# Graph and expert layers on one core: one long fill behind every four row sends, shared units five a step, batch norm on ScalarE

## The chip, the cores and the metric

The kernel runs on one core of one Trainium2 chip. The metric is the device time of one execution in microseconds (us). Five engines work side by side, each with its own instruction stream: TensorE (PE; its weight loads are shown apart as PEld), VectorE (DVE), ScalarE (ACT), GpSimd (POOL) and SyncE (SP). They meet through semaphores: an instruction waits until a semaphore has reached a count, and when it is done it raises one.

## What is computed

Two layers work on a stream of 8192 tokens of 128 numbers (128 batches of 64 nodes), each with a graph part and a feed-forward part. Cut to what matters:

```python
x = x + _L0_gnn_ref(_layernorm(x), adj, ...)      # eigenvectors of a 64x64 Laplacian
x = x + _L0_ffn_ref(_layernorm(x), ...)           # top 2 of 8 experts, silu gate
x = x + _L1_gnn_ref(_layernorm(x), adj, ...)      # batch norm over all tokens, twice
x = x + _L1_ffn_ref(_layernorm(x), ...)           # shared expert + top 2 of 8, gelu

# end of _L1_gnn_ref
out = h @ W2.T + b2
out = _batchnorm(out, g2, be2)
# _L1_ffn_ref
shared = gelu(x @ W1s + b1s) @ W2s + b2s
return shared + routed
```

## The kernel before

All arithmetic is float32. The tokens are kept in SBUF as 64 columns of 128 tokens (N = 64); four columns make a tile (PAIRS = 4, 512 tokens), so there are TILES = 16 tiles. Everything is written out by hand for each engine, with counted semaphores; no scheduler moves anything, so the order of an engine's code is its order on the chip.

The program runs in stages. First the eigenvectors of the Laplacian are found (to about 290 us of the profile). Then comes the graph part of layer 0, `gnn0_*`, to about 430 us; the experts of layer 0, `experts_*`; the graph part of layer 1 up to its first and second batch norm, `mix_*` and `out_*`; then `gnn1_*`, from about 870 to 1071 us; and the experts of layer 1, with the last stores.

**Routing and sends.** During `gnn0_*` and `gnn1_*` the tokens are normalised, their router logits are made, and a `Router` picks two experts for each token. It works on groups of GQ = 8 columns, two tiles, so there are GROUPS = 8 groups in each layer. `choose` and `place` on DVE give every token its row in a list in DRAM that is sorted by expert. `scatter` on POOL then sends the group: eight indirect DMAs (`send`, L1017), one for each column, of 128 rows of 1040 bytes. Behind every two sends stands a fill, a memset of a buffer `idle` that nobody reads (128x200 numbers, REST = 200, L1013). It raises `route_rested`, and each fill first waits for the fill before it. In the last group of layer 0 no fill stands between the eight sends, one stands behind them. When all 64 sends of a layer have landed, SP loads the rows expert by expert (L1482).

**Between the graph part and the experts of layer 0** PE has little to do: it sums the counts (`sum_counts`, L1098), runs five matmuls whose result nobody reads (`keep_warm`, L1409), spreads the limits of the routing table (`spread_limits`, L1105), runs six more, waits for the fill behind the last send, runs five more, and then turns the first rows of the experts (`turn_in`, L1641).

**`gnn1_*` goes in steps**, one for each tile, and then some more. In step s:

- DVE applies the second batch norm to tile s+1 of `OUT1` (`affine`, L1995, out `mgm`, semaphore `a1_gm`), adds the transposed tile s to the tokens (L2016), and works out the mean and inverse root of each token (`row_stats`, `inverse_root`, L2033). Among these it does `choose` or `place` of a group, and for the first EARLY = 4 tiles it adds the shared expert's result (`add_shared`, L2002).
- PE transposes the batch-normed tile s (L1919), transposes the normalised tile s-1 (L1936), makes its logits (L871), and works off shared units between these, in thirds.
- ACT normalises tile s (L1963), copies the transposed tile s-1 out of PSUM (L1974), and does the units' gelu (L1896).

A shared unit is one eighth of the shared expert for one tile. Four of the eight are *up* (one 128x512 product, L1875, followed by a gelu on ACT), four are *down* (four 128x128 products, L1882). There are 128 units; eight are kept for the gap in the middle of the experts, and 120 are done in `gnn1_*`, RATE = 6 in each step, from step 2 on: units 6(s-2) to 6(s-1). That makes A1_STEPS = 22 steps (0 to 21). A *down* unit needs its gelu, and an *up* unit needs the gelu of the unit two before it.

The sends of group g can start in step 2g+5; those of groups 0 and 1 also need the shared results of their tiles to be added.

Of the kernel before, what the change touches and what calls it, by code (L numbers as in the profile page):

```python
# [8 lines left out]
ALU = mybir.AluOpType  # L9
ACT = mybir.ActivationFunctionType  # L10
# [722 lines left out]
TILES = 16  # L733
PAIRS = 4
TOK = PAIRS * P
# [6 lines left out]
GQ = 8  # L742
REST = 200
GROUPS = N // GQ
# [87 lines left out]
def per_q(ap):  # L832
# [4 lines left out]
ROUTED = dict(lg=TILES, lg_free=GROUPS, carried=GROUPS, rank=GROUPS, slots=2 * GROUPS, shift=GROUPS, gap=GROUPS, exp=2 * GROUPS,  # L837
              picked=GROUPS, gates=GROUPS, rested=GQ // 2 * (GROUPS - 1) + 1, total=1, limits=1, limit_row=1, first=1)
SENT = 16 * N
# [8 lines left out]
class Router:  # L848
# [149 lines left out]
    def scatter(self, pool, g, xs, ready):  # L998

        pool.wait_ge(self.s("slots"), self.past("slots", 2 * (g + 1)))  # L1000
        pool.wait_ge(self.s("gates"), self.past("gates", (g + 1) * (1 + self.layer)))
        ready(g)
        for k in range(GQ // 2):
            for q in range(g * GQ + 2 * k, g * GQ + 2 * k + 2):
                self.send(q, xs).then_inc(self.s("sent"), 16)
            n = GQ // 2 * g + k
            if self.layer == 0 and g == GROUPS - 1:
                if k + 1 < GQ // 2:
                    continue
                n = GQ // 2 * g  # L1010
            if n or self.layer:
                pool.wait_ge(self.s("rested"), self.past("rested", n))
            self.nc.gpsimd.memset(self.t["idle"], 0.0).then_inc(self.s("rested"), 1)  # L1013

# [391 lines left out]
def keep_warm(nc, t, bank, n):  # L1406

    for _ in range(n):
        nc.tensor.matmul(bank[:, :], t["ident"], t["spin"], start=True, stop=True)  # L1409
# [422 lines left out]

RATE = 6
EARLY = 4
HELD = 1
UNITS = 2 * CH1 * TILES
AHEAD = UNITS - 2 * CH1 * HELD
A1_STEPS = 2 + -(-AHEAD // RATE)
PLACED = TILES + 2


def units(s):

    return range(max(0, RATE * (s - 2)), min(AHEAD, max(0, RATE * (s - 1))))


def thirds(todo):

    n = -(-len(todo) // 3)
    return todo[:n], todo[n:2 * n], todo[2 * n:]  # L1850
# [55 lines left out]
def gnn1_pe(nc, pe, S, t, ps, route):  # L1906
    T = nc.tensor
# [5 lines left out]
    for s in range(A1_STEPS):  # L1913
# [11 lines left out]
        if s == PLACED + 3:  # L1925
            route.spread_limits(pe)
        begin, middle, end = thirds(units(s))
        for n in begin:
# [18 lines left out]
def gnn1_act(nc, act, S, t, ps, route):  # L1947
    A = nc.scalar
# [4 lines left out]
    def keep(n):  # L1953
        i, k, rising, c = unit(n)
        if i >= EARLY and k == 2 * CH1 - 1:
            keep_shared(nc, act, S, t, ps, i)

    def normalised(T):
        if T >= TILES:
# [5 lines left out]
        ins.then_inc(S("a1_xh"), 1)  # L1965

    for s in range(A1_STEPS):
        begin, middle, end = thirds(units(s))
        for n in begin:
# [9 lines left out]
        for n in end:  # L1979
            gelu(n)  # L1980
        normalised(s)
        for n in units(s - 1):
            keep(n)
# [4 lines left out]
def gnn1_dve(nc, dve, own, S, t, ps, route):  # L1988
    V, X = nc.vector, t["X"]

    def affine(T):

        if T >= 2:
            dve.wait_ge(S("a1_t1"), T - 1)
        V.tensor_scalar(t["mgm"][T % 2], t["OUT1"][:, T * TOK:(T + 1) * TOK], t["bn2"][:, 0, 0:1], t["bn2"][:, 1, 0:1],  # L1995
                        ALU.mult, ALU.add).then_inc(S("a1_gm"), 1)

# [9 lines left out]

    dve.wait_ge(S("bn2_ready"), 1)
    affine(0)
    for s in range(A1_STEPS):  # L2010
        if s + 1 < TILES:
            affine(s + 1)
        if s < TILES:
# [78 lines left out]
def build(nc, d, out, tokens_out, scratch):  # L2092

    with ExitStack() as ctx:
# [134 lines left out]
        def _(pe):  # L2229
# [3 lines left out]
            routes[0].sum_counts(pe)  # L2233
            keep_warm(nc, t, ps[2], 5)
            routes[0].spread_limits(pe)
            keep_warm(nc, t, ps[2], 6)
            pe.wait_ge(S("route_rested"), GQ // 2 * (GROUPS - 1) + 1)
            keep_warm(nc, t, ps[2], 5)
            experts_pe(nc, pe, S, views[0], ps, 0)
# [98 lines left out]
```

## Time and profile before

| | us |
|---|---|
| median of 3 runs | 1388.89 |
| lowest and highest | 1387.36, 1392.39 |
| the profiled execution | 1388.02 |
| its span, first to last instruction | 1385.8 |
| PE busy in the span | 1137.4 (82%) |
| DVE busy | 922.1 (67%) |
| ACT busy | 565.5 (41%) |
| POOL busy | 511.5 (37%) |

The span is what the profile covers; 2.2 us of the profiled execution lie around it. Times in rows are us from the start of the span. Busy times count an engine's work, not its waits. A row's last part in brackets is how long the engine stood idle before it, and what released it: another engine's instruction, "issue" (nothing that the profile shows), or "remote", which is also called "another core or an unknown queue" (a semaphore that rose at a time that no instruction's end explains).

### The profile page before, as it was taken

To read this page: it belongs to the slowest core of one execution; us is meant where nothing else is said; L and a number is where in the kernel's file an instruction comes from. 1 tells how busy PE (TensorE), PEld (TensorE's weight loads), DVE (VectorE), ACT (ScalarE), POOL (GpSimd) and SP (SyncE) were. 2 spreads that over 40 slices of the span, in tenths; PEclk is the share of its full clock that TensorE was granted. 3 is DMA by queue.
4 is the path that set the end of the run, shared out by engine and by line. 5 is a ranking of instruction groups with operands and counts; after the bars stand their busy time and mean duration, and the time that the engine had idled before them with its cause. 6 is when DMAs were issued, how large, how long until landed. Compare 5 with 4: busy or idle time off the path is not lost.

```text
span 1385.8 us, 25378 instructions
## 1 busy us (share of the span) xinstructions
PE 1137.4 (82%) x7088; PEld 954.0 (69%) x7088; DVE 922.1 (67%) x3893; ACT 565.5 (41%) x1720; POOL 511.5 (37%) x586
## 2 busy tenths in 40 slices
PE   3555677268875999999999999796778999999992
PEld 3555577146653888978889654574556999989991
DVE  5777688858675566756668697884632566746673
ACT  2556657215540222212222367453433444544451
POOL 2100000053566345434444450025552455535561
PEclk9999999999886999999999999898979999999996
DMA  9999990000113334323232520001112344233326
GB/s 218 427 428 427 426 388 8 0 0 24 70 70 108 125 124 126 111 68 101 93 95 62 158 112 12 3 32 62 62 62 93 117 141 138 73 113 114 107 62 190
DMA packets 78348, 178.49 MB, mean 129 GB/s; under 512 B 11736, under 2 KB 51683, under 8 KB 75392
## 3 DMA queue, kind: packets, MB, share of 16 engines
q0 software_dynamic: 20544, 112.80, 20.5%
q1 hardware_dynamic: 51328, 60.92, 15.9%
q10 hardware_dynamic: 6336, 3.15, 0.8%
q8 instruction: 58, 0.95, 0.3%
q14 instruction: 82, 0.67, 0.2%
HBM read 60.91 MB, written 119.08 MB: 130 GB/s over the span
## 4 chain that ended last, share of the span: by engine, by line
PE 63%; DVE 16%; issue 10%; another core or an unknown queue 3%; ACT 3%; POOL 1%; DMA 1%; SPq 1%; DVEq 0%; POOLq 0%; ACTq 0%
PE bank L1669 17%; PE bank L1655 16%; PE bank L1658 6%; PE bank L195 4%; PE bank L1875 3%; PE bank L1882 3%; PE bank L1641 2%; PE bank L1818 2%; PE bank L1409 1%; PE bank L871 1%; DVE bnh L1719 1%; DVE u L180 1%; DVE u L171 1%; DVE u L166 1%
## 5 line engine op out<-in xcount | busy, mean ns | idle before, releaser
L1655 PE MATMUL bank<-work,wide 128*128 128x256 f32 (+3 forms) x994 | 215.4, 330 | 3.8 <-issue 2.3
L1669 PE MATMUL bank<-wide,work 128*128 128x128 f32 x1512 | 216.5, 278 | 1.1 <-DVE work L1591 1.0
L1669 PEld LDWEIGHTS bank<-wide,work 128*128 128x128 f32 x1512 | 198.0, 191 | 10.6 <-DVE work L1591 4.2
L1017 POOL DMA_INDIRECT rows<-tokens,slot x128 | 126.8, 990 | 172.8 <-issue 95.5
L1612 ACT ACTIVATE work<-bank 128x256 f32<-128x256 f32 (+1 forms) x216 | 82.7, 383 | 264.2 <-PE bank L1658 237.3
L1655 PEld LDWEIGHTS bank<-work,wide 128*128 128x128 f32 (+1 forms) x994 | 154.1, 186 | 16.8 <-DVE wide L1527 3.4
L1506 POOL DMA_INDIRECT rows<-wide x100 | 105.6, 1056 | 127.1 <-DVE wide L1543 105.9
L195 PE MATMUL bank<-u 63*64 63x2 f32 (+61 forms) x496 | 73.7, 255 | 66.3 <-DVE u L180 65.3
L195 PEld LDWEIGHTS bank<-u 63*64 63x64 f32 (+61 forms) x496 | 64.4, 217 | 71.8 <-DVE u L180 70.5
L1591 DVE TENSOR_TENSOR work<-work,bank 128x256 f32<-128x256 f32 (+1 forms) x216 | 87.9, 417 | 38.8 <-ACT work L1612 34.7
L1527 DVE COPY wide<-wreg 128x1066 f32 (+1 forms) x142 | 100.7, 709 | 16.4 <-issue 13.1
L1658 PE MATMUL bank<-work,wide 128*128 128x256 f32 (+3 forms) x426 | 105.3, 329 | 0.0
L1882 PE MATMUL bank<-wreg,work 128*128 128x128 f32 x512 | 72.8, 292 | 29.3 <-ACT work L1896 23.3
L1882 PEld LDWEIGHTS bank<-wreg,work 128*128 128x128 f32 x512 | 67.0, 204 | 40.9 <-ACT work L1896 29.6
L1621 ACT ACTIVATE work<-bank,wide 128x256 f32<-128x256 f32 x148 | 65.3, 475 | 73.1 <-PE bank L1655 71.0
L1538 DVE COPY work<-bank 128x256 f32<-128x256 f32 x144 | 60.4, 420 | 42.0 <-PE bank L1641 24.8
L1896 ACT ACTIVATE work<-bank,wreg 128x512 f32<-128x512 f32 x64 | 43.7, 688 | 102.4 <-PE bank L1875 57.9
L1669 PE MATMUL bank<-u,work 128*128 128x128 f32 (+1 forms) x504 | 77.8, 278 | 0.4 <-DVE work L1591 0.4
L1655 PE MATMUL bank<-work,u 128*128 128x256 f32 (+1 forms) x322 | 75.2, 335 | 1.2 <-issue 1.2
L1658 PEld LDWEIGHTS bank<-work,wide 128*128 128x128 f32 (+1 forms) x426 | 69.0, 178 | 8.5
L1506 POOL DMA_INDIRECT plane<-wide x50 | 49.7, 993 | 65.4 <-DVE wide L1543 55.8
L1506 POOL DMA_INDIRECT out<-wide x50 | 52.9, 1058 | 51.4 <-DVE wide L1543 41.6
(442 smaller groups left out, 2488.0 us busy)
## 6 DMA issues: line engine op xcount, KB each, us to landing
rows<-wide POOLq DMA_DIRECT2D x20, 3432.0 KB, 97.0
wide<-rows SPq DMA_DIRECT2D x100, 260.0 KB
wide<-rows SPq DMA_DIRECT2D x88, 130.0 KB
wreg<-in_w SPq DMA_DIRECT2D x1, 4264.0 KB, 25.2
wreg<-in_w SPq DMA_DIRECT2D x1, 4112.0 KB, 14.1
tokens<-in_x SPq DMA_DIRECT2D x2, 2048.0 KB, 20.1
tokens<-plane SPq DMA_DIRECT2D x16, 256.0 KB, 5.2
tokens<-out SPq DMA_DIRECT2D x12, 256.0 KB, 6.1
```

Source lines behind the costliest of these rows:

```text
L195: T.matmul(out, A[0:rows, col:col + 1].to_broadcast([rows, N]), rhs, start=True, stop=True).then_inc(hp, 1)
L1017: return self.nc.gpsimd.indirect_dma_start(out=xs, out_offset=bass.IndirectOffsetOnAxis(ap=self.t["slot"][:, q:q + 1], axis=0), in_=self.t ...
L1506: nc.gpsimd.indirect_dma_start(out=out, out_offset=bass.IndirectOffsetOnAxis(ap=goal, axis=0), in_=t["xin"][j % RING][:, h, 0:width], in_o ...
L1527: V.tensor_copy(t["wst"][n % WAYS][:, 0:WB[layer]], W[:, bass.ds(expert * WB[layer], WB[layer])]).then_inc(s("w"), 1)
L1538: V.tensor_copy(t["xte"][j % 2], ps[6][:, 0:TS]).then_inc(s("xt"), 1)
L1591: V.tensor_tensor(t["hh"][c][0:w, :], t["hs"][c][0:w, :], ps[c][0:w, TS:2 * TS], ALU.mult).then_inc(s("hh"), 1)
L1612: A.activation(t["hs"][c][0:w, :], ps[c][0:w, 0:TS], ACT.Silu).then_inc(s("hs"), 1)
L1621: A.activation(t["hh"][c], ps[c][:, 0:TS], ACT.Gelu, bias=bias[0]).then_inc(s("hh"), 1)
L1655: ins = T.matmul(ps[c][0:n, to], w[:, a:a + n], x[:, to], start=True, stop=True)
L1658: ins = T.matmul(ps[c][0:n, to3], w[:, HID0 + a:HID0 + a + n], x[:, to], start=True, stop=True)
L1669: ins = T.matmul(ps[4 + j % 2][:, h * P:(h + 1) * P], t["hh"][c][0:n, h * P:(h + 1) * P], w[0:n, at + c * P:at + (c + 1) * P], start=(c == ...
L1882: ins = nc.tensor.matmul(ps[4 + 2 * (i % 2)][:, q * P:(q + 1) * P], t["sh"][c][:, q * P:(q + 1) * P], t["WS"][:, (CH1 + c) * P:(CH1 + c + ...
```

## The change

It has four parts.

1. **Fills.** TOGETHER = 4: a fill stands behind every four sends, and it is 128x400 (REST = 400). POOL now waits for this fill itself before it goes on. In the last group of layer 0 there is no long fill; a fill of 128x8 stands behind the sixth send, and it is the one that PE waits for.
2. **Warm matmuls of layer 0.** The five before `spread_limits` and the five behind the wait are gone; six are left, behind the wait.
3. **Shared units.** RATE = 5, and units start in step 1: units 5(s-1) to 5s. In step 1 all five stand behind the logits. A1_STEPS is 25 (0 to 24).
4. **Batch norm.** `affine` moves from DVE to ACT as an activation with scale and bias. ACT does tiles 0 and 1 before step 0, and tile s+2 behind normalising tile s.

```diff
-REST = 200
+REST = 400
+TOGETHER = 4
...
-        for k in range(GQ // 2):
-            for q in range(g * GQ + 2 * k, g * GQ + 2 * k + 2):
+        for k in range(GQ // TOGETHER):
+            for q in range(g * GQ + TOGETHER * k, g * GQ + TOGETHER * (k + 1)):
                 self.send(q, xs).then_inc(self.s("sent"), 16)
-            n = GQ // 2 * g + k
-            if self.layer == 0 and g == GROUPS - 1:
-                if k + 1 < GQ // 2:
-                    continue
-                n = GQ // 2 * g
-            if n or self.layer:
-                pool.wait_ge(self.s("rested"), self.past("rested", n))
-            self.nc.gpsimd.memset(self.t["idle"], 0.0).then_inc(self.s("rested"), 1)
+                if self.layer == 0 and q == GROUPS * GQ - 3:
+                    self.nc.gpsimd.memset(self.t["idle"][:, 0:8], 0.0).then_inc(self.s("rested"), 1)
+            if self.layer == 1 or g + 1 < GROUPS:
+                self.nc.gpsimd.memset(self.t["idle"], 0.0).then_inc(self.s("rested"), 1)
+                pool.wait_ge(self.s("rested"), self.past("rested", GQ // TOGETHER * g + k + 1))
...
-RATE = 6
+RATE = 5
...
-A1_STEPS = 2 + -(-AHEAD // RATE)
+A1_STEPS = 1 + -(-AHEAD // RATE)
...
-    return range(max(0, RATE * (s - 2)), min(AHEAD, max(0, RATE * (s - 1))))
+    return range(max(0, RATE * (s - 1)), min(AHEAD, max(0, RATE * s)))
...
+    todo = units(s)
+    n = 0 if s == 1 else -(-len(todo) // 3)
     return todo[:n], todo[n:2 * n], todo[2 * n:]
...
+    def affine(T):
+        if T >= TILES:
+            return
+        if T >= 2:
+            act.wait_ge(S("a1_t1"), T - 1)
+        A.activation(t["mgm"][T % 2], t["OUT1"][:, T * TOK:(T + 1) * TOK], ACT.Identity, bias=t["bn2"][:, 1, 0:1],
+                     scale=t["bn2"][:, 0, 0:1]).then_inc(S("a1_gm"), 1)
...
         normalised(s)
+        affine(s + 2)
...
             routes[0].sum_counts(pe)
-            keep_warm(nc, t, ps[2], 5)
             routes[0].spread_limits(pe)
+            pe.wait_ge(S("route_rested"), GQ // TOGETHER * (GROUPS - 1) + 1)
             keep_warm(nc, t, ps[2], 6)
-            pe.wait_ge(S("route_rested"), GQ // 2 * (GROUPS - 1) + 1)
-            keep_warm(nc, t, ps[2], 5)
```

POOL's order at the end of layer 0's sends and at the start of layer 1's (`rows<-tokens,slot` is a send, `idle` a fill). Before:

```order
L1017 DMA rows<-tokens,slot 67584x260 x2
L1013 MEMSET idle 128x200
L1017 DMA rows<-tokens,slot 67584x260 x8
L1013 MEMSET idle 128x200
L1506 DMA rows<-wide 67584x260 x50
```

Now:

```order
L1015 DMA rows<-tokens,slot 67584x260 x4
L1010 MEMSET idle 128x400
L1015 DMA rows<-tokens,slot 67584x260 x6
L1008 MEMSET idle 128x8
L1015 DMA rows<-tokens,slot 67584x260 x2
L1504 DMA rows<-wide 67584x260 x50
```

The fill that PE waits for stands two sends earlier, and elsewhere four sends stand in a row.

PE's order around the routing table of layer 0. Before:

```order
L1098 MATMUL bank5<-carry,consts 128x16
L1409 MATMUL bank2<-consts 128x512 x5
L1105 MATMUL bank5<-tb,consts 128x94
L1409 MATMUL bank2<-consts 128x512 x11
```

Now:

```order
L1096 MATMUL bank5<-carry,consts 128x16
L1103 MATMUL bank5<-tb,consts 128x94
L1407 MATMUL bank2<-consts 128x512 x6
```

Ten of the sixteen warm matmuls are gone, five of them from behind the limits.

ACT's order from the normalising of step 2 of `gnn1_*` to that of step 3 (L1896, now L1895, is a gelu; L1974, now L1984, the copy out of PSUM). Before:

```order
L1963 ACTIVATE tokens<-tokens,norm 128x128 x4
L1974 COPY u1<-bank1 128x512
L1896 ACTIVATE work<-bank2,wreg 128x512
L1896 ACTIVATE work<-bank3,wreg 128x512
L1896 ACTIVATE work<-bank2,wreg 128x512
L1963 ACTIVATE tokens<-tokens,norm 128x128 x4
```

Now:

```order
L1970 ACTIVATE tokens<-tokens,norm 128x128 x4
L1962 ACTIVATE work<-u1,bn2 128x512
L1895 ACTIVATE work<-bank2,wreg 128x512
L1984 COPY u1<-bank1 128x512
L1895 ACTIVATE work<-bank3,wreg 128x512
L1970 ACTIVATE tokens<-tokens,norm 128x128 x4
```

The batch norm (L1962) stands right behind the normalising, ahead of the gelus of the next step.

## Rows read from the trace of the kernel before

**Rows 1.** Chain of work, 868 to 1080 us: shares by line; start, us, what.
```profile
by line: PE bank L1875 21.2%; PE bank L1882 20.7%; another core or an unknown queue 18.9%; ACT tokens L1963 6.1%; PE bank L871 5.6%; issue 5.4%; PE bank L1936 3.3%; ACT work L1896 2.8%; PE bank L1919 2.0%; PE bank L1655 1.7%; PE bank L1669 
...
886.40 0.89 PE bank L1882 x8
887.29 0.86 PE bank L1875 x2
...
918.63 3.42 another core or an unknown queue
```

**Rows 2.** Busy us (instructions) of PE, PEld, DVE, ACT, POOL; clock, DMA share, GB/s.
```profile
926.00:937.00 11.00, 10.50 (x69) 8.03 (x68) 9.52 (x49) 5.46 (x12) 0.00 (x0) 1.00 0.03 9
...
947.00:960.00 13.00, 1.75 (x6) 0.48 (x4) 0.00 (x0) 1.16 (x3) 9.97 (x14) 0.63 0.29 104
```

**Rows 3.** PE in time: transposes that open steps 5, 6, 10, 11.
```profile
905.44 0.60 PE L1919 MATMUL bank<-consts,work 128*128 128x128 f32 x4
...
912.85 0.60 PE L1919 MATMUL bank<-consts,work 128*128 128x128 f32 x4
...
944.85 0.60 PE L1919 MATMUL bank<-consts,work 128*128 128x128 f32 x4
...
966.95 0.60 PE L1919 MATMUL bank<-consts,work 128*128 128x128 f32 x4
```

**Rows 4.** DVE in time: start, us, line, shapes, idle before and releaser.
```profile
946.10 0.68 DVE L1995 TENSOR_SCALAR work<-u,bn 128x512 f32<-128x512 f32 x1 [0.68 <-DVE norm L2034]
960.25 0.69 DVE L2016 TENSOR_TENSOR tokens<-tokens,bank 128x512 f32<-128x512 f32 x1 [13.46 <-remote]
```

**Rows 5.** POOL in time: sends (L1017) and fills (L1013) of layer 1.
```profile
914.93 1.02 POOL L1017 DMA_INDIRECT rows<-tokens,slot  x1 [43.94 <-ACT tokens L1963]
...
939.64 0.29 POOL L1013 MEMSET idle<- 128x200 f32 x1
940.09 0.97 POOL L1017 DMA_INDIRECT rows<-tokens,slot  x1 [0.17 <-issue]
941.36 0.97 POOL L1017 DMA_INDIRECT rows<-tokens,slot  x1 [0.30 <-issue]
942.33 0.29 POOL L1013 MEMSET idle<- 128x200 f32 x1
...
945.55 0.97 POOL L1017 DMA_INDIRECT rows<-tokens,slot  x1 [0.17 <-issue]
...
958.56 0.29 POOL L1013 MEMSET idle<- 128x200 f32 x1
```

**Rows 6.** DVE in time, layer 0, under sends without fills.
```profile
436.62 0.17 DVE L1072 SCALAR_TENSOR_TENSOR tb<-tb,kroute 128x16 f32<-128x16 f32 x1
437.67 0.19 DVE L1074 TENSOR_TENSOR tb<-tb 128x32 f32<-128x32 f32 x1 [0.88 <-DVE tb L1072]
```

**Rows 7.** PE in time, layer 0: limits, warm matmuls, first expert tile.
```profile
441.91 0.74 PE L1105 MATMUL bank<-tb,consts 128*128 128x94 f32 x2 [7.39 <-DVE tb L1082]
442.44 10.96 PE L1409 MATMUL bank<-consts 128*128 128x512 f32 x22
453.24 0.38 PE L1641 MATMUL bank<-consts,wide 128*128 128x128 f32 x2
```

**Rows 8.** SP in time: the first row loads of the experts.
```profile
445.78 3.64 SPq L1482 DMA_DIRECT2D wide<-rows  x4
```

**Rows 9.** Busy us per stretch, columns as in the windows above.
```profile
447.50:448.50 1.00, 1.00 (x3) 0.38 (x2) 0.31 (x1) 0.00 (x0) 0.00 (x0) 1.00 0.59 135
...
441.90:445.00 3.10, 3.09 (x5) 1.60 (x6) 0.48 (x2) 0.00 (x0) 2.01 (x3) 0.50 0.35 129
```

**Rows 10.** POOL by line: the long fill, count, busy us, mean ns.
```profile
L714 POOL MEMSET work<- 128x868 f32 x1 | 0.8, 822 | 173.6 <-DMA rows<-wide 173.6
```

**Rows 11.** Source lines: count, ns min/median/max, first and last start, form.
```profile
L1807 ACT ACTIVATE work<-u,bn x16: 797/798/801, 838.8 to 862.9; 128x512 f32<-128x512 f32 x16
...
L1995 DVE TENSOR_SCALAR work<-u,bn x16: 530/546/680, 870.7 to 995.2; 128x512 f32<-128x512 f32 x16
```

More of the change, by code:

```diff
@@ L837 @@
 ROUTED = dict(lg=TILES, lg_free=GROUPS, carried=GROUPS, rank=GROUPS, slots=2 * GROUPS, shift=GROUPS, gap=GROUPS, exp=2 * GROUPS,
-              picked=GROUPS, gates=GROUPS, rested=GQ // 2 * (GROUPS - 1) + 1, total=1, limits=1, limit_row=1, first=1)
+              picked=GROUPS, gates=GROUPS, rested=GQ // TOGETHER * (GROUPS - 1) + 1, total=1, limits=1, limit_row=1, first=1)
 SENT = 16 * N
@@ L1837, with thirds @@
 AHEAD = UNITS - 2 * CH1 * HELD
-A1_STEPS = 2 + -(-AHEAD // RATE)
+A1_STEPS = 1 + -(-AHEAD // RATE)
 PLACED = TILES + 2
 def units(s):
-    return range(max(0, RATE * (s - 2)), min(AHEAD, max(0, RATE * (s - 1))))
-def thirds(todo):
-    n = -(-len(todo) // 3)
+    return range(max(0, RATE * (s - 1)), min(AHEAD, max(0, RATE * s)))
+def thirds(s):
+    todo = units(s)
+    n = 0 if s == 1 else -(-len(todo) // 3)
     return todo[:n], todo[n:2 * n], todo[2 * n:]
@@ L1926, in gnn1_pe @@
             route.spread_limits(pe)
-        begin, middle, end = thirds(units(s))
+        begin, middle, end = thirds(s)
         for n in begin:
@@ L1965, in normalised @@
         ins.then_inc(S("a1_xh"), 1)
+    act.wait_ge(S("bn2_ready"), 1)
+    affine(0)
+    affine(1)
     for s in range(A1_STEPS):
-        begin, middle, end = thirds(units(s))
+        begin, middle, end = thirds(s)
         for n in begin:
@@ L1989, in gnn1_dve @@
     V, X = nc.vector, t["X"]
[L1991 to L1996, printed above, removed]
     def add_shared(i):
@@ L2006, in root @@
             inverse_root(V, dve, t, S("a1_inv"), s, k)
-    dve.wait_ge(S("bn2_ready"), 1)
-    affine(0)
     for s in range(A1_STEPS):
-        if s + 1 < TILES:
-            affine(s + 1)
         if s < TILES:
```

## The prediction, made before the changed kernel ran

> **What bounds the kernel now.** I read the chain of waits first, then windows, then single engines in time. The change touches three places: the sends of both layers, PE between the graph part and the experts of layer 0, and `gnn1_*`.
>
> In `gnn1_*` the chain of waits between 868 and 1080 us is mostly PE: *up* products L1875 hold 21.2%, *down* products L1882 20.7% [rows 1]. The surprise is the third entry, "another core or an unknown queue" with 18.9% of these 212 us, that is 40 us [rows 1]. It is time in which an engine waits for a semaphore whose producer has long finished. One place shows it plainly. PE ends the transposes of step 10 within 0.6 us of 944.85 [rows 3]; DVE, which waits for just these, starts L2016 at 960.25, after 13.46 us idle, released by "remote" [rows 4]. From 947 to 960 us DVE does nothing, ACT 1.16 us and PE 1.75 us of work, while POOL is busy for 9.97 of 13 us [rows 2]. POOL sends in this time without a break, until its fill at 958.56 [rows 5], and 1.4 us behind the end of this fill everybody moves on. From 926 to 937 us, where POOL sends nothing, PE is busy for 10.50 of 11 us [rows 2]. So semaphores that PE raises arrive late while POOL sends, and this costs 40 us. It does not set in at once: the burst that starts at 914.93 [rows 5] shows its first such wait at 918.63 [rows 1], 3.7 us later, in the third send. What it is in the chip the trace does not say.
>
> Without sends a step lasts as long as PE's work: 905.44 to 912.85 is 7.41 us for six units [rows 3]. With sends, step 10 to 11 takes 22.1 us (944.85 to 966.95) [rows 3].
>
> In layer 0 the start of the experts hangs on PE's warm matmuls. The limits are out at about 442.6, eleven warm matmuls (22 records) fill PE to 453.24, and only then the first rows are turned [rows 7]. The loads of these rows were issued from 445.78 on, 1.1 us apart [rows 8], and the DMA engines' share dips at 447.5 to 448.5, between the first and the second load [rows 9]; I take 448.5 for the landing of the first.
>
> **Part 2, warm matmuls.** Six are left. PE ran the first four records at half clock, since the clock is 0.50 from 441.90 to 445.00 [rows 9], and the other 18 in 453.24 - 445.06 = 8.2 us [rows 7], 0.45 us each. Twelve records then end at 445.06 + 8 x 0.45 = 448.7, just after the first load. The wait for the small fill behind the sixth send costs nothing: that send is over at about 441.4, before the limits. The experts' first turn moves from 453.2 to 448.9: **-4.3 us**. Cover is the load: if the sends end later, this gain shrinks by as much beyond 0.3 us. PE is the bound of the experts, so what starts earlier ends earlier. The five warm matmuls ahead of the limits did not keep the clock up (it was at half when PE came back [rows 9]), so their removal costs nothing.
>
> **Part 1, POOL's time.** A pair costs one fill-to-fill distance, 942.33 - 939.64 = 2.69 us, so four sends 5.38 [rows 5]. Now: a send takes 0.97 and the gap behind it 0.30, behind a fill 0.17 [rows 5]. The long fill lies between 0.29 (200 numbers) [rows 5] and 0.82 (868) [rows 10]; on the line through both, 400 numbers take 0.45. Four sends are 4 x 0.97 + 3 x 0.30 + 0.45 + 0.17 = 5.40, plus up to 0.15 for waiting for the fill itself: 5.5. For eight sends that is +0.0 to +0.3. In layer 0 the last three groups run back to back; two of them have fills, so the last send comes 0 to 0.5 us later, which the warm matmuls mostly hide: 0.1 us.
>
> **Part 1, late semaphores.** This is the large and uncertain term. The quiet time between two sends becomes 0.45 + 0.17 + up to 0.15 = 0.6 to 0.8 us once in four sends, instead of 0.46 once in two [rows 5]. No row shows a pause of this length inside a burst, so I bound it. In favour: a fresh burst is free of trouble for 3.7 us. If the longer pause resets it, each quartet of 5.5 us is exposed for only 1.8 us; 16 quartets give 29 us at most, against 40: -11, and a quartet's last stall ends with its pause instead of running on for 13 us, so I take -13. End on the good side: nearly all 40 us go, of which PE could use 30. Against: the waits went on for 1.4 us behind the last fill [rows 4, 5], longer than the new pause, so it may reset nothing: 0. Worse: in layer 0 the last eight sends run without fills, and there even DVE's own semaphore is late: L1072 is over at 436.8, and L1074, which needs nothing else, starts at 437.67, after 0.88 us [rows 6], in the third send since a fill. If every quartet does this to DVE, 30 quartets (14 in layer 0, 16 in layer 1) cost 26 us, of which half lies on the chain: +13. I take -13, since the pause is longest where the stall is longest, and the range spans -30 to +13.
>
> **Parts 3 and 4.** PE's work is the same 120 units; an *up* takes 0.86, a *down* 0.89 [rows 1]. A step with five units needs 7.41 - 0.88 = 6.5 us of PE. DVE is busy for 9.52 of 11 us [rows 2], 6.4 us of a 7.41 us step; without the affine (0.546 us, x16 [rows 11]) 5.9. So DVE no longer holds a shorter step back, though in steps with `choose` and `add_shared` it comes close. ACT gets 0.80 us more per step (L1807, the same shape and operands' kind [rows 11]): it has 5.46 of 11 us [rows 2], 3.7 per step, so 4.5 of 6.5. But the activation stands behind the normalising, in front of the gelus of the next step, and one *down* in eight waits for such a gelu. I put 0.2 us on each of 16 steps, +3 in sum, between 0 (ACT's slack hides it) and 0.5 per step (+8). The early start at step 1 gains the 0.9 us that PE's first units had to wait for the next transposes, and loses about as much, since tile 2's transposes and the normalising of tile 1 now stand behind five cold units: 0. The eight steps behind the last tile are pure PE work that was there before.
>
> The Trainium skill, page "SBUF — State Buffer", section "Who interferes with whom", says that a VectorE copy or tensor_scalar in a 2-port mode holds a port pair exclusively, and that GpSimd's descriptor writing is fully blocked meanwhile. By that rule, moving `affine` off DVE would free POOL by up to 16 x 0.55 = 9 us. The trace disagrees in the one overlap shown: the send at 945.55 takes 0.97 us as the others do, though L1995 starts at 946.10 inside it [rows 4, 5]; it is DVE that grows, to 0.68. The sum takes nothing from it.
>
> **Sum.** Against the profiled execution's own 1388.0 (0.9 under the median of 1388.9): -4.3 + 0.1 + 0 + 3 - 13 = -14.2, so 1373.8; against the median 1374.7. **Forecast: 1375.**
>
> **Rivals.**
> *The pause resets nothing* (B). Then late semaphores cost 40 us as before, and -4.3 + 0.1 + 3 gives 1387.7. For it: semaphores were late for longer behind the last fill than the pause lasts. Against: some pass in the middle of a burst.
> *Four sends in a row are worse than two* (C), the slower side. DVE loses 0.88 us in each of 30 quartets, from the third send on; half of 26 us on the chain, 1387.7 + 13 = 1401. It decides from about 0.1 us per quartet on the chain upwards. For it: rows 6. Against: that stretch had no pause at all.
> *ACT becomes the bound of `gnn1_*`* (D): 0.5 us in each of 16 steps is +8 in place of +3, on top of A or B: 1380 or 1393. For it: the place in front of the gelus; against: ACT is at 70% of the shorter step at most.
>
> **How the numbers follow.** A (resets, the forecast) 0.45, spread from 1358 (all of it gone) to 1382; B 0.28, 1384 to 1392; C 0.19, 1392 to 1410; D with B 0.08, 1393. A measurement of this kernel can tell about 0.5% from no change, 6.9 us: faster is below 1382, slower above 1395.8. Faster: A without its edge and a little of B, 0.48. Slower: most of C and a part of D, 0.2. Same: the rest, 0.32. The range leaves out the ends of A and the far part of C: 1359 to 1398. A's own range is 1362 to 1382.
>
> **What would show it.** Warm matmuls: the first turn of the experts (L1641, now two lines less) near 449 instead of 453.2. Late semaphores: in `gnn1_*` the share of "another core or an unknown queue" falls from 40 us to below 27, and no wait of DVE for the transposes lasts over 5 us; in B and C it stays, in C DVE shows waits of 0.9 us for itself in third and fourth sends, and the graph part of layer 0 grows. Steps: quiet steps of `gnn1_*` of 6.5 to 6.8 us; 7 us or more, with PE waiting for ACT's gelu, means D. The fill should take 0.45 us. The forecast falls first if the long pause is still too short.

## The result, and the profile of the changed kernel

| first comparison, us | before | changed |
|---|---|---|
| median | 1389.07 | 1344.71 |
| lowest to highest | 1387.36 to 1392.39 | 1343.04 to 1352.95 |
| the profiled execution | 1388.02 | 1343.91 |
| its span | 1385.8 | 1342.1 |

The ratio is 0.969 (95% interval 0.9646 to 0.9733): 44 us less, where 14 were forecast, and below the range. The experiments then added a second result, which is the more important one. The kernel *before* does not always take 1389 us. On most occasions it takes 1336 us, and there the changed kernel is 0.8% **slower** (1.0080, 1.0043 to 1.0117). Both results are told here.

The page of the changed kernel, first lines:

```profile
span 1342.1 us, 25322 instructions
...
PE 1111.7 (83%) x7068; PEld 937.9 (70%) x7068; DVE 915.1 (68%) x3877; ACT 576.0 (43%) x1736; POOL 507.2 (38%) x556
```

The chain of waits in the window of [rows 1], 868 to 1080 us, shares by line:

```profile
by line: PE bank L1874 19.8%; PE bank L1881 19.4%; PE bank L1667 10.9%; PE bank L1653 10.7%; PE bank L872 4.6%; issue 3.7%; ACT tokens L1970 2.9%; PE bank L1935 2.4%; PE bank L1918 2.4%; DVE bn L1148 2.1%; DVE tokens L2016 1.6%; PE bank L16
```

"Another core or an unknown queue", 18.9% of this window before [rows 1], is not in the list any more. The experts' lines (L1653, L1667) have come into it, since they begin at 1030.3 and no longer at 1071.6.

POOL in time: the last two of four sends (L1015), the fill (L1010), and the next send; then PE's transposes (L1918) and DVE's add that waits for them, at the same place:

```profile
914.01 0.97 POOL L1015 DMA_INDIRECT rows<-tokens,slot  x1 [0.30 <-issue]
915.29 0.97 POOL L1015 DMA_INDIRECT rows<-tokens,slot  x1 [0.31 <-issue]
916.25 0.46 POOL L1010 MEMSET idle<- 128x400 f32 x1
917.51 0.97 POOL L1015 DMA_INDIRECT rows<-tokens,slot  x1 [0.80 <-issue]
```

```profile
915.75 0.60 PE L1918 MATMUL bank<-consts,work 128*128 128x128 f32 x4
```

```profile
917.18 0.69 DVE L2016 TENSOR_TENSOR tokens<-tokens,bank 128x512 f32<-128x512 f32 x1 [0.74 <-PE bank L1918]
```

PE is done at 916.35 and DVE starts at 917.18, 0.83 us later: PE's semaphore is still late. But the fourth send ends at 916.26, the next starts at 917.51, and DVE goes on inside this pause of **1.25 us**, 0.92 us behind the send's end. Before, the longest wait of this kind lasted 13.46 us [rows 4]. The pause is twice what I had worked out: POOL's wait for its own fill costs 0.80 us, not 0.17 plus up to 0.15.

The table follows both profiled executions.

| us in the span | before | changed | difference |
|---|---|---|---|
| last send of layer 0 ends | 443.93 | 440.62 | -3.3 |
| first expert turn, layer 0 | 453.24 | 445.69 | -7.6 |
| `gnn1_*` opens (L1919, now L1918) | 871.42 | 864.57 | -6.9 |
| first expert turn, layer 1 | 1071.61 | 1030.32 | -41.3 |
| end of the span | 1385.8 | 1342.1 | -43.7 |

So 34.4 of the 43.7 us come out of `gnn1_*` (200.2 us before, 165.8 now), 7.6 out of the time up to the first turn of layer 0.

### The profile page after: what moved, and what is told of

Its sections match the earlier page's. It is cut to its first block, busy times and chain, and to the rows that moved or that the text cites. A ratio compares the mean times of both kernels' runs of the same rounds, so it can differ in the third digit from the quotient of the medians.

```text
span 1342.1 us, 25322 instructions
## 1 busy us (share of the span) xinstructions
PE 1111.7 (83%) x7068; PEld 937.9 (70%) x7068; DVE 915.1 (68%) x3877; ACT 576.0 (43%) x1736; POOL 507.2 (38%) x556
## 4 chain that ended last, share of the span: by engine, by line
PE 62%; DVE 20%; issue 10%; ACT 2%; DMA 2%; POOL 1%; SPq 1%; DVEq 0%; another core or an unknown queue 0%; POOLq 0%; ACTq 0%
PE bank L1667 17%; PE bank L1653 16%; PE bank L1656 6%; PE bank L195 4%; PE bank L1874 3%; PE bank L1881 3%; PE bank L1639 2%; PE bank L1816 2%; DVE bnh L1717 1%; DVE u L180 1%; DVE u L171 1%; PE bank L389 1%; DVE u L166 1%; DVE tokens L1298 1%; DVE bn L1115 1%
## 5 line engine op out<-in xcount | busy, mean ns | idle before, releaser
L1667 PE MATMUL bank<-wide,work 128*128 128x128 f32 x1512 | 216.5, 278 | 1.1 <-DVE work L1589 1.0
L1653 PE MATMUL bank<-work,wide 128*128 128x256 f32 (+3 forms) x994 | 215.3, 330 | 2.2 <-DVE work L1536 1.4
L1667 PEld LDWEIGHTS bank<-wide,work 128*128 128x128 f32 x1512 | 198.1, 191 | 10.5 <-DVE work L1589 4.0
L1015 POOL DMA_INDIRECT rows<-tokens,slot x128 | 125.5, 981 | 139.0 <-ACT tokens L1970 47.5
L1653 PEld LDWEIGHTS bank<-work,wide 128*128 128x128 f32 (+1 forms) x994 | 154.1, 186 | 14.7 <-issue 1.8
L1536 DVE COPY work<-bank 128x256 f32<-128x256 f32 x144 | 60.4, 420 | 43.7 <-PE bank L1639 27.7
L1881 PEld LDWEIGHTS bank<-wreg,work 128*128 128x128 f32 x512 | 64.3, 193 | 23.2 <-issue 14.3
L1667 PE MATMUL bank<-u,work 128*128 128x128 f32 (+1 forms) x504 | 77.8, 278 | 0.5 <-DVE work L1589 0.5
L1653 PE MATMUL bank<-work,u 128*128 128x256 f32 (+1 forms) x322 | 75.1, 335 | 1.4 <-issue 1.4
L1881 PE MATMUL bank<-wreg,work 128*128 128x128 f32 x512 | 69.2, 281 | 4.3 <-issue 2.2
L1667 PEld LDWEIGHTS bank<-u,work 128*128 128x128 f32 (+1 forms) x504 | 68.7, 191 | 4.1 <-DVE work L1589 2.1
```

The source lines that it names most:

```text
L1015: return self.nc.gpsimd.indirect_dma_start(out=xs, out_offset=bass.IndirectOffsetOnAxis(ap=self.t["slot"][:, q:q + 1], axis=0), in_=self.t ...
L1536: V.tensor_copy(t["xte"][j % 2], ps[6][:, 0:TS]).then_inc(s("xt"), 1)
L1653: ins = T.matmul(ps[c][0:n, to], w[:, a:a + n], x[:, to], start=True, stop=True)
L1667: ins = T.matmul(ps[4 + j % 2][:, h * P:(h + 1) * P], t["hh"][c][0:n, h * P:(h + 1) * P], w[0:n, at + c * P:at + (c + 1) * P], start=(c == ...
L1881: ins = nc.tensor.matmul(ps[4 + 2 * (i % 2)][:, q * P:(q + 1) * P], t["sh"][c][:, q * P:(q + 1) * P], t["WS"][:, (CH1 + c) * P:(CH1 + c + ...
```

## The experiments

### Two kinds of occasion

The first four kernels undid or isolated parts of the change. Each set ran beside the kernel before on one chip.

`fills_undone`: the changed kernel without part 1 (one line of it shown).

```
-            for q in range(g * GQ + TOGETHER * k, g * GQ + TOGETHER * (k + 1)):
+            for q in range(g * GQ + 2 * k, g * GQ + 2 * k + 2):
```

> The changed kernel with part 1 (the fills) undone: 128x200 behind every two sends, each waiting for the fill before it, one fill behind the last eight sends of layer 0. Parts 2 to 4 stay. Theory P (the pause between sends is what lets late semaphores land: with the changed kernel's own wait it is 1.25 us, the delayed ones land 0.8 to 0.9 us behind a send's end, and a pause of 0.46 us is too short): the late semaphores are back, 'another core or an unknown queue' takes 30 to 40 us of the chain in gnn1_*, time 1380 to 1390. Rival Q (the lighter DVE and the shorter steps removed them): 1343 to 1352, share near 0.

`fills_alone`: the kernel before with the fills of the changed kernel.

> The kernel before with part 1 (the fills) alone: 128x400 behind every four sends, waited for by POOL, 128x8 behind the sixth of the last eight sends of layer 0. Theory P: 1348 to 1356, gnn1_* 34 us shorter, the first expert turn of layer 0 some 2 to 4 us earlier than before. Rival Q: within 5 us of the kernel before, 1384 to 1392.

`units_affine_undone`: the changed kernel with RATE = 6, units from step 2 on, and `affine` back on DVE.

> The changed kernel with parts 3 and 4 undone: six units a step from step 2 on, batch norm applied by DVE. Theory P with PE as the bound of gnn1_*: PE's work is the same, so 1344 to 1350. Rival Q: the late semaphores are back, 1370 or more. Rival D turned round (the activation on ACT costs): up to 5 us faster than the changed kernel, 1340.

`no_own_wait`: the changed kernel without POOL's wait behind the fill.

```
+                if self.layer or g or k:
+                    pool.wait_ge(self.s("rested"), self.past("rested", GQ // TOGETHER * g + k))
                 self.nc.gpsimd.memset(self.t["idle"], 0.0).then_inc(self.s("rested"), 1)
-                pool.wait_ge(self.s("rested"), self.past("rested", GQ // TOGETHER * g + k + 1))
```

> The changed kernel, but POOL does not wait for a fill behind it; each fill waits for the one before it, as in the kernel before. Fills stay at 128x400 behind four sends, so the pause between sends shrinks from 1.25 to about 0.62 us. Theory P with its threshold at 0.8 to 0.9 us: late semaphores of over 5 us are back, 1360 to 1385. Rival R (a long fill in four sends is enough, whatever the pause): 1342 to 1346, with sends that end earlier.

Measured, with the kernel before at **1335.6 us** beside them: `fills_undone` 1344.4 (ratio 1.0054, 1.0038 to 1.0071), `fills_alone` 1339.5 (1.0029, 1.0013 to 1.0046), `units_affine_undone` 1342.3 (1.0034, 1.0008 to 1.0060), `no_own_wait` 1340.6 (1.0028, 1.0006 to 1.0050). No kernel showed a late semaphore, and none could tell theory P from a rival. My expectations had no place for a kernel before at 1336. In `fills_undone` something else shows: all its warm matmuls stand behind the fill of the last send, and its first turn of layer 0 comes 8.6 us behind that send's end, where the kernel before needs 4.75 (`before_again`). Its time is thus not that of parts 3 and 4 alone.

So the two kernels themselves ran again, beside each other.

> The kernel before, unchanged, run once more with its profile. In the first comparison it took 1389 us with 40 us of late semaphores in gnn1_*; beside the four experiments it took 1336 us, and none of these four showed a late semaphore. Theory S (late semaphores belong to the chip or its state in the first comparison, not to the kernel alone): two kinds of occasion only, 1336 us with a share of 'another core or an unknown queue' near 0 in gnn1_*, or 1389 us with 40 us of it. Rival K (something in the kernel's own timing decides from run to run): times in between, and both kinds within one set of runs.

> The changed kernel, unchanged, on the same chip as before_again. On an occasion without late semaphores (before at 1336): 1340 to 1346, that is 0.3 to 0.8% slower than the kernel before, since parts 3 and 4 alone (fills undone) cost 0.5%, and 1 to 2 late semaphores at most. On an occasion with them (before at 1389): 1345, and each is over within 0.9 us of a fourth send's end.

Measured: before 1334.9 (all its runs on this occasion 1336.1), changed 1347.3 (1.0080, 1.0043 to 1.0117), a little above the 1340 to 1346 expected. The chain of the kernel before, 868 to 1080 us, on this occasion:

```profile
by line: PE bank L1875 23.7%; PE bank L1882 22.4%; PE bank L1655 12.3%; PE bank L1669 11.8%; PE bank L871 6.1%; ACT tokens L1963 5.3%; PE bank L1936 4.0%; issue 2.4%; PE bank L1919 1.9%; PE bank L1641 1.6%; ACT work L1896 1.0%; PE bank L954
```

The same program, and the 18.9% of [rows 1] are gone. POOL sends as in [rows 5], with the same pauses of 0.46 us, and DVE waits 1.29 us in the midst of them, for work of PE that was really late:

```profile
941.82 0.97 POOL L1017 DMA_INDIRECT rows<-tokens,slot  x1 [0.30 <-issue]
942.78 0.29 POOL L1013 MEMSET idle<- 128x200 f32 x1
943.24 0.97 POOL L1017 DMA_INDIRECT rows<-tokens,slot  x1 [0.17 <-issue]
944.51 0.97 POOL L1017 DMA_INDIRECT rows<-tokens,slot  x1 [0.30 <-issue]
```

```profile
945.07 0.69 DVE L2016 TENSOR_TENSOR tokens<-tokens,bank 128x512 f32<-128x512 f32 x1 [1.29 <-PE bank L1919]
```

DVE's waits for itself in layer 0 [rows 6] are gone too: L1072 starts at 433.11 and L1074 at 433.31. `gnn1_*` takes 159.7 us instead of 200.2. Theory S stands, K falls: over all occasions the kernel before had a median of 1332 to 1337 us (seven occasions) or of 1389 to 1409 us (four, with the first comparison), and never one between (on two of the four late occasions one single run stood far above the rest, at 2830 and 2283 us; why is not known). I call them **quiet** and **late** occasions. Whether a late one is a property of a chip, of its neighbours or of something that ran before is not settled: chip numbers stand beside the runs; one number stood with 1336 us twice and with 1389 us once, another was late both times.

### Which part removes the late semaphores

Only a late occasion can answer this, and only four more kernels met one. The first two:

`warm_alone`: the kernel before with part 2 alone.

> The kernel before with part 2 alone: six warm matmuls instead of sixteen, all behind a fill that stands behind the sixth of layer 0's last eight sends. On an occasion without late semaphores (before at 1336): the two differences seen so far (units_affine_undone less fills_alone, 2.8 us; changed kernel less no such pair) say +2 to +4 us, 1338 to 1340, from a half clock in the first expert tiles; rival: 0, since both kernels turn the first rows about 5 us behind the last send. On an occasion with late semaphores (before at 1389): 1382 to 1388, their 40 us in gnn1_* untouched.

`no_fills`: the kernel before without fills, but for the last of layer 0.

> The kernel before without any fill between sends; only the one behind the last send of layer 0, which PE waits for, stays. On an occasion without late semaphores: 1333 to 1336, the same as before or 1 to 3 us faster, and still none is late: then fills are worth nothing there. If fills are what keeps them away even there, late semaphores of PE over 5 us and 1350 or more. On an occasion with them: over 1400.

Measured, with the kernel before at 1390.8: `warm_alone` 1390.2 (0.9982, 0.9953 to 1.0010), `no_fills` 1401.7 (1.0088, 1.0053 to 1.0124). The fills of before are thus worth 11 us on such an occasion, far less than the 53 us at stake. "Another core or an unknown queue" has 21.3% of the same window in `warm_alone` and 17.0% in `no_fills`; these shares don't order the two, since the other waits grow with them.

In `warm_alone` the place of part 2 is seen by itself, PE in time:

```profile
438.01 0.74 PE L1105 MATMUL bank<-tb,consts 128*128 128x94 f32 x2 [9.28 <-issue]
441.74 7.87 PE L1409 MATMUL bank<-consts 128*128 128x512 f32 x12 [2.98 <-issue]
449.45 0.38 PE L1641 MATMUL bank<-consts,wide 128*128 128x128 f32 x2
```

The first turn comes at 449.45, though the last send ends later than before (444.1 instead of 443.9). That is the forecast place and size, but the wait for the fill is not free: PE stands idle for 2.98 us before the six matmuls, which start as this fill ends (441.68). The whole did not get faster by part 2: 1382 to 1388 was expected, and `gnn1_*` took 207 us in this execution, 7 more than in the first profile.

`no_own_wait_alone`: the kernel before with the long fill behind every four sends, not waited for. `short_fill_alone`: with a fill of 128x8 that is waited for.

```
-REST = 400
+REST = 8
```

> The kernel before with 128x400 behind every four sends, which POOL does not wait for (pause 0.62 us), and nothing else of the change. On an occasion without late semaphores: 1334 to 1337, as the kernel before, 3 us less than fills_alone if the own wait is what part 1 costs there. On an occasion with them: theory P 1360 to 1389, rival R 1340.

> The kernel before with a fill behind every four sends that POOL waits for itself, as in part 1, but of 128x8 instead of 128x400. The pause between sends becomes about 0.14 + 0.80 = 0.94 us instead of 1.25 us. On an occasion without late semaphores (before at 1336 us): 1336 to 1338, 2 us less than fills_alone, since each of 30 pauses is 0.3 us shorter. On an occasion with them (before at 1389): theory P (a pause of 0.8 to 0.9 us or more lets them land) 1338 to 1346; rival R (it is the length of the fill that counts) over 1365.

> The same kernel as no_own_wait (long fill behind four sends, pause 0.62 us instead of 1.25 us). Without late semaphores: 1340 as before. With them: theory P (the pause must outlast 0.8 to 0.9 us) says 1360 to 1385; rival R (any long fill does) says 1345.

> The same kernel as no_own_wait_alone: the kernel before with 128x400 behind every four sends, not waited for by POOL, so the pause between sends is 0.62 us. Beside it the kernel before shows which kind of chip this is. On a chip with late semaphores (before at 1389 us): theory P (the pause must outlast the 0.8 to 0.9 us by which a late one lands behind a send's end) says 1360 to 1395 and waits of over 5 us in gnn1_*; rival R (one long fill in four sends is enough) says 1335 to 1345. On a chip without them (before at 1336 us) both say 1336.

These fell on quiet occasions: `no_own_wait_alone` 1.0002 (0.9979 to 1.0026) and 1.0019 (0.9992 to 1.0046), `short_fill_alone` 1.0012 (0.9983 to 1.0042), `no_own_wait_2` 1.0032 (1.0008 to 1.0056). The first was as expected (1336.1), `short_fill_alone` (1339.8) was above the 1336 to 1338. The price of the own wait on a quiet occasion is not told apart from the spread of the medians: `fills_alone` and `fills_alone_2` cost 0.6 to 3.9 us, and within the changed kernel it is 5.4 us between the medians of one occasion (1347.3 with the wait, 1341.9 in `no_own_wait_2`), with intervals that overlap. The next run fell on a late occasion.

> The kernel before with 128x400 behind every four sends, not waited for by POOL (pause 0.62 us), once more, for a chip with late semaphores (before at 1389 us): theory P 1360 to 1395 with waits of over 5 us in gnn1_*, rival R 1335 to 1345. On a chip without them both say 1336.

Measured, with the kernel before at 1409.4: 1406.6 (0.9999, 0.9969 to 1.0029). **The long fill alone does nothing.** (The time is above the 1360 to 1395 expected, as the kernel before itself was above 1389 here.) PE, POOL and DVE in time:

```profile
955.29 0.60 PE L1919 MATMUL bank<-consts,work 128*128 128x128 f32 x4
```

```profile
962.50 0.98 POOL L1017 DMA_INDIRECT rows<-tokens,slot  x1 [0.30 <-issue]
963.45 0.47 POOL L1013 MEMSET idle<- 128x400 f32 x1
964.09 0.97 POOL L1017 DMA_INDIRECT rows<-tokens,slot  x1 [0.17 <-issue]
965.37 0.97 POOL L1017 DMA_INDIRECT rows<-tokens,slot  x1 [0.30 <-issue]
966.64 0.97 POOL L1017 DMA_INDIRECT rows<-tokens,slot  x1 [0.30 <-issue]
967.92 0.97 POOL L1017 DMA_INDIRECT rows<-tokens,slot  x1 [0.30 <-issue]
968.88 0.45 POOL L1013 MEMSET idle<- 128x400 f32 x1
```

```profile
970.77 0.69 DVE L2016 TENSOR_TENSOR tokens<-tokens,bank 128x512 f32<-128x512 f32 x1 [11.99 <-remote]
```

PE's transposes are done at 955.89. DVE waits through the pause of 0.62 us at 963.5 and is let go only at 970.77, 1.9 us behind the end of the last send (968.89), much as in [rows 4, 5].

> The same kernel as fills_alone: the kernel before with part 1 alone (128x400 behind every four sends, waited for by POOL, pause 1.25 us). On a chip with late semaphores (before at 1389 us or more; the kernel with a pause of 0.62 us took 1407 us there): theory P says 1336 to 1345, the share of 'another core or an unknown queue' in gnn1_* below 2%, and every late semaphore over within 1 us of a send's end. Rival (the pause helps only together with parts 3 and 4, which lighten DVE and thin the steps): 1360 or more. On a chip without them: 1339, as before.

> The same kernel as fills_alone_2, which fell on a chip without late semaphores: part 1 alone. On a chip with them (before at 1389 us or more): theory P 1336 to 1345 and every late semaphore over within 1 us of a send's end; rival (only together with parts 3 and 4) 1360 or more. On a chip without: 1336 to 1340.

`fills_alone_2` fell on a quiet occasion (1336.2, ratio 1.0017, 0.9992 to 1.0041). `fills_alone_3`, beside the kernel before at 1389.2: **1343.9** (0.9673, 0.9597 to 0.9750). Part 1 alone brings the whole gain of the first comparison. It has two runs only (1348.4 and 1339.5), but both lie over 40 us below all three of the kernel before beside it. Its chain, 868 to 1080 us:

```profile
by line: PE bank L1873 24.2%; PE bank L1880 24.1%; PE bank L1653 10.6%; PE bank L1667 10.1%; PE bank L872 6.2%; issue 5.3%; PE bank L1934 4.3%; ACT tokens L1961 3.0%; PE bank L1917 2.6%; PE bank L1639 1.4%; ACT work L1894 1.4%; PE bank L955
```

`gnn1_*` takes 160.8 us here, where it took 200.2: 39.4 us less, all of the 40 us of [rows 1].

Was the profiled execution of `fills_alone_3` late at all, or had the trouble gone by itself? The traces record when each semaphore rises. The table counts those in `gnn1_*` that rose over 1 us after the end of the instruction that raises them:

| trace | pause | over 1 us late | longest, us |
|---|---|---|---|
| `before`, first comparison | 0.46 behind two sends | 25 | 14.8 |
| `warm_alone` | 0.46 behind two | 23 | 13.3 |
| `no_fills` | none | 24 | 15.2 |
| `no_own_wait_alone_3` | 0.62 behind four | 26 | 15.2 |
| the changed kernel, first comparison | 1.25 behind four | 9 | 2.1 |
| `fills_alone_3` | 1.25 behind four | 3 | 1.3 |
| the other 14 traces | all kinds | 0 | none late |

So semaphores were late in `fills_alone_3` too; part 1 does not remove them but cuts them short. Where they landed inside a pause of 1.25 us, in this trace and in that of the changed kernel, it was 0.80 to 1.06 us behind the last send's end, when a pause of 0.62 us is already over. In `fills_alone_3` two land at 965.78 and 965.87, in the pause between these sends:

```profile
963.83 0.98 POOL L1015 DMA_INDIRECT rows<-tokens,slot  x1 [0.30 <-issue]
964.78 0.48 POOL L1010 MEMSET idle<- 128x400 f32 x1
966.06 0.98 POOL L1015 DMA_INDIRECT rows<-tokens,slot  x1 [0.80 <-issue]
```

That speaks for the length of the pause. But part 1 with and without the own wait differs in two things, the length and the wait itself, and no run on a late occasion separates them; `short_fill_alone` was made for it and never met one. Nor did a kernel with parts 3 and 4 but the old fills meet one: part 1 is shown to be enough, not to be the only part that could do it.

To place the threshold between 0.62 and 1.25 us, the short fill ran twice more.

> The same kernel as short_fill_alone: the kernel before with 128x8 behind every four sends, waited for by POOL, pause 0.94 us. On a chip with late semaphores (before at 1389 us): late ones land 0.80 to 0.97 us behind a send's end in the changed kernel's trace, so a pause of 0.94 us lets most but not all through: 1338 to 1350, and some waits run over a pause. If the threshold is nearer 1.25 us, they are back: 1365 or more. On a chip without: 1336 to 1340.

> The same kernel as short_fill_alone_2, which fell on a chip without late semaphores. On a chip with them (before at 1389 us): threshold at or below 0.94 us 1338 to 1350, threshold above it 1365 or more. On a chip without: 1336 to 1342.

Both fell on quiet occasions (1.0076, 1.0018 to 1.0134, from three runs, its 1342.5 us above the 1336 to 1340 expected; and 0.9989, 0.9961 to 1.0018). The threshold **stays open**.

### What the rest of the change costs

`affine_dve`: the changed kernel with part 4 alone undone.

> The changed kernel with part 4 alone undone: DVE applies the batch norm, units stay at five a step from step 1. With part 3 and 4 undone together gnn1_* (first transposes to first expert turn of layer 1) took 159.6 us, with both 165.8. Theory D (ACT's activation in front of the gelus costs): gnn1_* near 160, time 4 to 6 us below the changed kernel. Rival U (the thin steps of five units with their eight steps behind the last tile cost): gnn1_* near 166, time as the changed kernel.

Measured: 1344.1, a ratio to the kernel before of 1.0062 (1.0033 to 1.0091), where the changed kernel beside it had 1.0080 (1.0043 to 1.0117); these overlap. `gnn1_*` on quiet occasions, one trace each:

| | length of `gnn1_*`, us | PE busy | PE idle |
|---|---|---|---|
| six units a step (9 traces) | 157.3 to 159.7 | 144.6 to 147.0 | 12.7 to 12.8 |
| five units, batch norm on DVE (`affine_dve`) | 163.2 | 148.0 | 15.2 |
| both parts (`fills_undone`, `no_own_wait`, `no_own_wait_2`) | 162.7 to 162.9 | 147.5 to 147.7 | 15.1 to 15.2 |
| both parts (`after_again`) | 165.4 | 150.0 | 15.4 |

That is rival U: the steps of five units cost 3 us or more (4.9 between `fills_alone`, 157.8, and `fills_undone`, 162.7), and with the batch norm on ACT as well nothing is added in three traces of four. In the fourth, `after_again`, 2.0 of the 2.2 us over `affine_dve` are longer busy time of PE, not waits: the granted clock is 0.97 there from 978.8 us on, where `affine_dve` has 1.00. What made it fall in this one trace is not known.

Waits of PE from 862 to 1040 us, the rows that differ; first the kernel before (`before_again`), then the changed one (`after_again`), then `affine_dve`:

```profile
PE bank L1882 <- ACT u L1903: 4.9, 3, 2.4
```

```profile
PE bank L955 <- DVE rt L932: 4.7, 7, 1.3
PE bank L1881 <- ACT u L1902: 2.1, 2, 1.6
...
PE bank L1881 <- ACT work L1895: 0.8, 1, 0.8
```

```profile
PE bank L955 <- DVE rt L932: 6.0, 7, 1.5
```

L955 multiplies what `choose` leaves on DVE. With six units a step PE finds it ready (in the kernel before these waits are 0.1 us in sum); with five it waits seven times. That undoing part 4 makes this wait longer (6.0) fits it: DVE, not ACT, makes a short step wait. Busy us from `gnn1_*`'s opening to the third step's, before (`before_again`) and changed (`after_again`), columns as in [rows 2]:

```profile
865.10:884.90 19.80, 13.47 (x60) 9.46 (x61) 14.96 (x71) 7.79 (x14) 0.00 (x0) 0.74 0.00 1
```

```profile
868.30:886.10 17.80, 11.47 (x42) 7.82 (x43) 7.94 (x44) 6.86 (x12) 0.00 (x0) 0.62 0.00 0
```

The granted clock is 0.74 in the one and 0.62 in the other: of the two levels, the changed kernel spends more of this stretch at 1.2 GHz, and its first five units run in it. Over all of `gnn1_*` PE is busy for 147.0 us in this pair before and 150.0 changed, with the same work, and idle for 12.7 and 15.4: 3.0 us of slower work and 2.7 us of waits make the 5.7 us between the two. The table shows the waits in every trace. Of the slower work, both traces of this pair have a dip of the clock later on too (0.98 from 884.9 us in the one, 0.97 from 978.8 in the other), so a pair without one is the better measure: `fills_alone` 145.1 and `fills_undone` 147.6, both at 1.00 behind the first stretch (they differ in parts 1 and 2 too, which leave PE's work here alone). The difference of 2.5 us is nearly all in the shared units (L1873 and L1880 there, L1876 and L1883 here: 123.9 and 127.0 us).

## Why the prediction was wrong, point by point

**Late semaphores, the term that failed.** The mechanism was read rightly as far as it went: they come late while POOL sends, and a long enough pause with POOL's own wait lets them land. The term was put at -13 us; `gnn1_*` alone gave 34.4 in the first comparison and 39.4 in `fills_alone_3`. Two steps of its sizing failed.

First, the pause. "Plus up to 0.15 for waiting for the fill itself" was 0.63: the gap behind the waited fill is 0.80 us where it is 0.17 without the wait. The pause is 1.25 us, not 0.6 to 0.8. At the low end of my own range the change would have brought nothing: a pause of 0.62 us, without the own wait, is `no_own_wait_alone_3`, and there rival B is right. So it is luck that the direction came out: the pause was worked out too short. The step looked harmless because I priced it as POOL's time (+0.1); its worth was in the pause.

Second, what is left once the pause works. I left each quartet "exposed for only 1.8 us", 29 us in sum. In the traces the late ones last up to 2.1 us (the one behind the wait at 917.18 is 0.8 us late), but the chain loses next to nothing by them: of the 40 us 39.4 went (`fills_alone_3`). That PE has units in hand meanwhile is my explanation, not shown by a run. "-30" as the best end was therefore too small: I put 10 us of the 40 down as not usable. I also counted nothing in layer 0. By the medians of different occasions the whole price is 1389 - 1336 = 53 us, 13 more than `gnn1_*` has. How much of them is layer 0's is open: the first expert turn comes at 453.2 late and at 445.2 quiet, but it varies as much without late semaphores (443.8 to 452.2 over the 14 quiet traces), and in `fills_alone_3` it comes at 453.3 again. [Rows 6] showed a piece of it, and I had used them only for rival C.

**The kernel before is not one number.** I took its 40 us as its own. On a quiet occasion they don't exist, and the same change costs 0.8%. No row of the first trace could tell this; the sentence "what it is in the chip the trace does not say" was the place to put a rival: that it need not be there on another occasion.

**Warm matmuls, -4.3.** The place was right: 449.45 in `warm_alone`, forecast 448.9. (The working counts four records at half clock; the fourth starts at 445.06 and is the first quick one, which turns its 448.7 into 448.9.) What was wrong is that this gain exists on its own everywhere, and that the wait for the small fill "costs nothing". In the changed kernel the limits are out at 432, 6 us ahead of that fill (438.05), and PE stands idle for 5.55 us before the six matmuls:

```profile
438.24 7.61 PE L1407 MATMUL bank<-consts 128*128 128x512 f32 x12 [5.55 <-issue]
```

The first turn at 445.69 hangs on the sends, which end 3.3 us earlier than before; part 2 has no part in that. On a quiet occasion the kernel before turns 4.75 us behind its last send (440.43 to 445.18) and the changed one 5.0 us (442.46 to 447.46): the limits are out early there, the sixteen warm matmuls lie beside the sends, and nothing is left to gain. The medians of one quiet occasion even say +2.8 us for part 2 (1342.3 with parts 1 and 2, 1339.5 with part 1), about as much as such medians spread.

**POOL's time, +0.1.** The fill is 0.46 us (0.45 was worked out). A quartet takes 917.51 - 911.40 = 6.1 us, not 5.5, which is the own wait again. On a quiet occasion part 1 costs 0.6 to 3.9 us (`fills_alone_2`, `fills_alone`).

**Units and ACT, +3.** In size near, and by luck: the two parts cost `gnn1_*` some 5 us, inside 0 to 8. In mechanism wrong: the 3 us were for PE waiting for gelus behind the batch norm, and no share of ACT's can be told from zero; rival D is not it. "DVE no longer holds a shorter step back" failed in the steps with `choose` (L955), where PE waits 4.3 to 6.0 us in sum; other waits shrink, so PE's idle time grows by 2.4 to 2.7 us. And "0" for the early start left out that all five first units run mostly at the lower clock, 2.5 us in sum.

**DVE beside a send.** I took nothing for moving `affine` off DVE, from one overlap [rows 4, 5]. That stands: the sends have a median of 0.97 us with it on DVE and on ACT (`affine_dve`, `after_again`). But that overlap was a weak test of the rule cited there, since the send had begun first and it was DVE that grew, and no row shows that L1995 runs in the mode the rule speaks of. Better ones were in the same trace: three sends that began about 0.1 us after an L1995 took 0.97 to 0.98 us. (In `no_own_wait_alone` two of four such sends took 1.2 us; but so does one at 1004.90 in the changed kernel, where `affine` is on ACT.)

**Steps of 6.5 us** came: 888.16, 894.67 and then 901.92 with `choose` in it:

```profile
888.16 0.60 PE L1918 MATMUL bank<-consts,work 128*128 128x128 f32 x4
894.67 0.60 PE L1918 MATMUL bank<-consts,work 128*128 128x128 f32 x4
901.92 0.60 PE L1918 MATMUL bank<-consts,work 128*128 128x128 f32 x4
```

**Rival C** (quartets are worse) fell: in `gnn1_*` of the changed kernel DVE's longest wait for itself is 0.2 us. Its sign did show elsewhere: in `no_own_wait_alone_3`, four sends and a pause of 0.62 us, DVE waits 0.99 us for itself at 956.4, yet the kernel is no slower than before. And where there is no pause at all, in `no_fills`, DVE stands idle for 1.03 us before L1082, waiting for its own L1081:

```profile
446.51 0.29 DVE L1082 TENSOR_SCALAR tb<-consts,tb 128x128 f32<-128x128 f32 x1 [1.03 <-DVE tb L1081]
```

**The better version.** `fills_alone` has the gain of the changed kernel on a late occasion (1343.9, against 1344.7 in the first comparison) and costs 0.2 to 0.3% on a quiet one (1336.2 and 1339.5), where the changed kernel costs 0.8%. Parts 2 to 4 should be left out. No kernel here beats the kernel before on a quiet occasion by more than the noise.

## What to carry to other kernels

Idle time that a trace puts down to an unknown releaser may be the occasion's and not the kernel's: run the unchanged kernel again on other occasions before a change is credited with taking it away. Price a wait not only by what it costs its own engine but by the pause that it makes, for here 0.63 us of waiting in four sends came with a gain of 45 us, and the longer fill without it with none. A step with fewer units for the bound engine is shorter only if the other engines' work in it shrinks as well.

## What the runs showed of the hardware

- Semaphores of PE, and more seldom of DVE, can reach a waiting engine more than 13 us late while POOL issues indirect sends back to back, on some occasions only; on others none was late, with the same program and the same pauses.
- On late occasions a pause of 1.25 us behind four sends kept the delays to about 2 us, and pauses of 0.46 us behind two sends or 0.62 us behind four did not (up to 15 us). Whether the length counts or POOL's wait for its own semaphore is not separated.
- A fill of 128x400 that POOL waits for itself makes a pause of 0.46 + 0.80 us; without the wait 0.46 + 0.17 us.
